# A state-space mixer computed by batch halves behind its convolution

## The reference, cut to what matters

```
z, xs, Bs, Cs, dt = split(h @ w_in.T);  xBC = silu(conv(xs, Bs, Cs) + b)
a = dt * A;  cs = cumsum(a) in chunks of 128 tokens;  L = exp(cs_q - cs_k), causal
Yd = (C B^T * L) (x dt)            # inside a chunk
states = sum_q exp(cs_end - cs) B (x dt);  S <- g S + states, S = 0 at each sequence's start
Yo = C S_prev exp(cs)              # from the chunks before
y = (Yd + Yo + D x) * silu(z);  h = res + y @ w_out.T
h2 = h * rsqrt(mean(h*h) + eps) * ln2_w;  h + (silu(h2 gate^T) * (h2 up^T)) down^T
```

## Time and profile before

| | before |
|---|---|
| median of three runs | 2204.54 us |
| profiled execution | 2204.26 us, span 2202.4 us |
| TensorE / weight loads / VectorE / ScalarE / POOL busy | 96 / 77 / 76 / 48 / 8 % |
| TensorE's mean granted clock | 0.981 |
| DMA | 361.6 MB, mean 164 GB/s |
| chain that ended last, by engine | PE 82 %, DVE 12 %, ACT 3 %, issue 2 %, DMA 1 % |

### The profile page before, as it was taken

The page is one execution under the profiler, slowest core; times in us unless marked ns, Lnnn a source line. Parts: engine busy times, 40 slices in busy tenths (PEclk is TensorE's granted clock), DMA queues, the critical chain, the costliest instruction groups (busy, mean ns, idle before and its releaser), DMA issues.

```text
span 2202.4 us, 26828 instructions
## 1 busy us (share of the span) xinstructions
PE 2123.8 (96%) x9262; PEld 1687.1 (77%) x9266; DVE 1668.0 (76%) x2498; ACT 1051.5 (48%) x1710; POOL 174.8 (8%) x287
## 2 busy tenths in 40 slices
PE   7999998969999999999999999799999999999999
PEld 3787776847888887888888864578888888888887
DVE  7775566468777888887978888977777777689885
ACT  4333224226777777776444456533333333334442
POOL 0000110000111111111000000200000000000000
PEclk9999999979999999999999999899999999999999
DMA  3151002525889999989360032634454444665201
GB/s 120 39 189 41 28 29 95 134 34 169 298 297 311 321 341 333 315 307 373 112 220 1 1 144 83 176 137 167 148 180 150 151 172 146 232 229 183 86 19 58
DMA packets 132958, 361.61 MB, mean 164 GB/s; under 512 B 16288, under 2 KB 27168, under 8 KB 129184
## 3 DMA queue, kind: packets, MB, share of 16 engines
q1 hardware_dynamic: 108912, 279.78, 37.1%
q0 software_dynamic: 23920, 80.23, 10.6%
HBM read 279.73 MB, written 84.41 MB: 165 GB/s over the span
## 4 chain that ended last, share of the span: by engine, by line
PE 82%; DVE 12%; ACT 3%; issue 2%; DMA 1%; DVEq 0%; SPq 0%; ACTq 0%
PE pair L913 41%; PE pair L938 24%; PE pair L718 9%; DVE conv_out L1873 1%; PE pair L969 1%; DVE comb_lo L1624 1%; DVE ring_lo L1574 1%; PE pair L831 1%; DVE pair L1710 1%; PE pair L856 1%; PE pair L857 1%; PE pair L838 1%; PE pair L754 1%; PE pair L860 1%; PE pair L963 1%
## 5 line engine op out<-in xcount | busy, mean ns | idle before, releaser
L913 PE MATMUL pair<-comb_hi,ring_hi 128*128 128x512 f32 x1568 | 618.4, 394 | 34.7 <-DVE comb_lo L1621 12.4
L913 PE MATMUL pair<-comb_hi,ring_lo 128*128 128x512 f32 x1568 | 615.6, 393 | 0.0
L913 PE MATMUL pair<-comb_lo,ring_hi 128*128 128x512 f32 x1568 | 615.6, 393 | 0.0
L913 PEld LDWEIGHTS pair<-comb_hi,ring_hi 128*128 128x128 f32 x1568 | 297.8, 190 | 106.8 <-issue 22.9
L913 PEld LDWEIGHTS pair<-comb_hi,ring_lo 128*128 128x128 f32 x1568 | 297.7, 190 | 62.5
L913 PEld LDWEIGHTS pair<-comb_lo,ring_hi 128*128 128x128 f32 x1568 | 298.2, 190 | 61.5
L938 PE MATMUL pair<-inner_ring_a,ring_hi 128*128 128x512 f32 x1120 | 344.9, 389 | 0.0
L938 PEld LDWEIGHTS pair<-inner_ring_a,ring_hi 128*128 128x128 f32 x1120 | 210.1, 188 | 43.6
L938 PE MATMUL pair<-inner_ring_a,ring_lo 128*128 128x512 f32 x560 | 217.9, 389 | 0.0
L1158 ACT ACTIVATE ring_hi<-ring_sum 128x512 fp32r<-128x512 f32 x168 | 106.0, 631 | 147.0 <-DVE ring_sum L1561 145.2
L718 PE MATMUL pair<-act_hi,weights_hi 128*128 128x512 f32 x416 | 138.6, 414 | 12.2 <-DVE act_lo L1517 8.0
(11 more groups left out here) (340 smaller groups left out, 3191.5 us busy)
## 6 DMA issues: line engine op xcount, KB each, us to landing
coeff_in<-f_gu SPq DMA_DIRECT2D x56, 512.0 KB, 5.2
coeff_in<-b_gu SPq DMA_DIRECT2D x56, 512.0 KB, 6.8
weights_raw<-w_mamba SPq DMA_DIRECT2D x28, 512.0 KB, 3.3
raw_a<-w_gu SPq DMA_DIRECT2D x28, 512.0 KB, 6.8
raw_a<-w_gu SPq DMA_DIRECT2D x56, 256.0 KB, 6.3
u_spill<-gate_a POOLq DMA_DIRECT2D x56, 256.0 KB, 6.0
coeff_in<-f_dn SPq DMA_DIRECT2D x28, 512.0 KB, 4.5
coeff_in<-b_dn SPq DMA_DIRECT2D x28, 512.0 KB, 6.3
```

The costliest lines, as they stand in the source:

```text
L913: ins = pe.matmul(out, wt[:, slot, col], a, start=t in (0, 1, 3) and kk == 0 and n == 0, stop=kk == KH - 1 and n == 2, skip_group_check=True)
```

## The change

Everything from the gate projection to the root works on one batch half at a time, batch 1 first (ORDER = (1, 0)).

- Each weight block of the gate and the output projection is loaded and split twice, once for each half: 32 positions instead of 16. A chunk has two half blocks of its own batch; TensorE's half_step does three matmuls of 512 columns.
- The first chunk of a sequence leaves out the state (no decayed C, no product with it; the state is a copy), the last leaves out the new state and the transposes of B. The hardware loops are written out, and the copies of columns into cur go.
- Gate activations of batch 1 are done in chunk 4, its products and splits in chunks 5 to 7 (Y_AT). Batch 0's are made during the output blocks of batch 1.
- The output projection has 16 half blocks on four PSUM banks; residual reload and x_sum stores are by halves too.
- Squares, their sum, root and scale are per half. Batch 1's sum is taken behind block 9, its root at block 10, combinations 0 and 1 at blocks 11 and 13, the first four ring weights at block 14. Batch 0's root comes behind the last block, with its sum between the first two products of the feed-forward.
- act_hi, act_lo, the gate and the combinations get other places in memory (T_HI, T_LO).

The diff, cut to its core; of the loops that are replaced only the new text stands here, moved to the left:

```diff
-N_CONV, N_Z, N_OUT, N_MLP = 0, CONV_TILES, CONV_TILES + 8, CONV_TILES + 16
+N_CONV, N_Z, N_OUT, N_MLP = 0, CONV_TILES, CONV_TILES + 16, CONV_TILES + 32
+BLOCK_OF = list(range(CONV_TILES)) + 2 * list(range(CONV_TILES, CONV_TILES + 8)) + 2 * list(range(CONV_TILES + 8, CONV_TILES + 16))
+ORDER = (1, 0)
+Y_AT = {5: (0, 1, 2), 6: (3, 4, 5), 7: (6, 7)}
...
-    AH = at("act_hi", 0, [P, KT, TOK], F32R)
-    AL = at("act_lo", 32 * KB, [P, KT, TOK], F32R)
+    AH = at("act_hi", 0, [P, BATCH, KT, H], F32R)
+    AL = at("act_lo", 32 * KB, [P, BATCH, KT, H], F32R)
...
-    zg = at("z_gate", R0, [P, KT, TOK], F32)
+    zg = (at("z_gate_a", R0 + 16 * KB, [P, KT, H], F32), at("z_gate_b", R0, [P, KT, H], F32))
+    rms_scale = at("rms_scale", R0 + 16 * KB, [P, BATCH, H], F32)
+    rms_sq = at("rms_squares", R0 + 20 * KB, [P, 2, H], F32)
+    rms_sum = at("rms_sum", R0 + 24 * KB, [P, BATCH, H], F32)
+    rms_t = at("rms_steps", R0 + 28 * KB, [P, BATCH, H], F32)
...
-    T_HI = ((56, 96, 104, 112, 120, 176, 184), (0, 24, 80, 32, 176, 184, 48))
-    T_LO = ((0, 8, 16, 24, 32, 40, 48), (16, 8, 88, 56, 72, 64, 40))
+    T_HI = ((0, 8, 16, 48, 112, 176, 96), (0, 24, 80, 32, 176, 184, 48))
+    T_LO = ((32, 40, 24, 56, 120, 184, 104), (16, 8, 88, 56, 72, 64, 40))
...
-with sp.Fori(0, (N_MLP - 4) // 2) as i:
-    for s in range(2):
-        load(i * 2 + (4 + s), s, w_mamba[i * 2 + (4 + s)])
+for n in range(4, N_MLP):
+    load(n, n % 2, w_mamba[BLOCK_OF[n]])
...
-pool.dma_start(hres[:, :, :], hs_spill.rearrange("k p t -> p k t")).then_inc(s_reload, 16)
+for h, b in enumerate(ORDER):
+    pool.dma_start(hres[:, :, HALF[b]], hs_spill.rearrange("k p t -> p k t")[:, :, HALF[b]]).then_inc(s_reload[h], 16)
 pool.wait_ge(s_xcopy, 16)
-for o in range(KT):
-    pool.wait_ge(s_h, o + 1)
-    pool.dma_start(x_sum[o], hres[:, o, :], accum_op=ALU.add).then_inc(s_xsum, 16)
+for h, b in enumerate(ORDER):
+    for o in range(KT):
+        pool.wait_ge(s_h, h * KT + o + 1)
+        pool.dma_start(x_sum[o][:, HALF[b]], hres[:, o, HALF[b]], accum_op=ALU.add).then_inc(s_xsum, 16)
...
+def half_step(out, wi, b, k):
+    for n, (w, a) in enumerate(((WH, ah), (WH, al), (WL, ah))):
+        ins = pe.matmul(out, w[:, wi, k * P:(k + 1) * P], a(b, k),
+                        start=k == 0 and n == 0, stop=k == KT - 1 and n == 2, skip_group_check=True)
+    if k == KT - 1:
+        ins.then_inc(s_used, 1)
...
+def gate_steps(q, first, last):
+    for u in range(first, last):
+        s, k = divmod(u, KT)
+        if k == 0:
+            pe.wait_ge(s_ready, N_Z + 2 * q + s + 1)
+            if q > 0:
+                pe.wait_ge(s_z, 2 * q - 1 + s)
+        half_step(bank(s), s, ORDER[q // CHUNKS], k)
+for q in range(NC):
+    h, c = divmod(q, CHUNKS)
+    b = ORDER[h]
+    first = KT if c == 0 else 4
+    gate_steps(q, 0, first)
+    pe.wait_ge(s_conv, CONV_TILES + 2)
+    pe.wait_ge(s_csx, 2)
+    pe.wait_ge(s_rr, q + 1)
+    for g in range(GROUPS):
+        ins = pe.matmul(ps[1][:, g * 512:(g + 1) * 512], ones[:, :], cs_rhs[:, g * HPG:(g + 1) * HPG, :],
+                        start=True, stop=False, skip_group_check=True)
+    ins.then_inc(s_cs, 1)
+    pe.wait_ge(s_bx, q + 1)
+    pe.wait_ge(s_silu, CONV_TILES)
+    pe.wait_ge(s_yt, q + 1)
+    for g in range(GROUPS):
+        pe.matmul(ps[2][:, g * 512:(g + 1) * 512], bx_cur[:, 2 + g, :],
+                  xbc[:, 4 + g * HPG:4 + (g + 1) * HPG, b * SEQ + c * P:b * SEQ + (c + 1) * P],
+                  start=True, stop=True)
+    gate_steps(q, first, first + 2)
+    if c > 0:
+        pe.wait_ge(s_state, h * (CHUNKS - 1) + c)
+    for j in range(4 if c < CHUNKS - 1 else 2):
+        ins = pe.transpose(ps[3][:, j * P:(j + 1) * P], bx_cur[:, j, :], ident)
+    ins.then_inc(s_stage, 1)
+    gate_steps(q, first + 2, first + 4)
+    if c > 0:
+        pe.wait_ge(s_ecs, h * (CHUNKS - 1) + c)
+    for g in range(GROUPS):
+        ins = pe.matmul(ps[1][:, g * 512:(g + 1) * 512], ident_bf[:, :],
+                        mask_bf[:, :].unsqueeze(1).to_broadcast([P, HPG, P]),
+                        start=False, stop=True, skip_group_check=True)
+    ins.then_inc(s_msk, 1)
+    gate_steps(q, first + 4, 2 * KT)
+    pe.wait_ge(s_att, q + 1)
+    for hd in range(HEADS):
+        ins = pe.matmul(ps[2][:, hd * P:(hd + 1) * P], x_dt[:, hd, :], att[:, hd, :], start=True, stop=c == 0)
+        if c > 0:
+            ins = pe.matmul(ps[2][:, hd * P:(hd + 1) * P], state[:, hd, :], c_dec[:, hd, :], start=False, stop=True)
+    ins.then_inc(s_y, 1)
+    if c < CHUNKS - 1:
         for g in range(GROUPS):
             ins = pe.matmul(ps[3][:, g * 512:(g + 1) * 512], b_tm[:, g, :], x_end[:, g * HPG:(g + 1) * HPG, :],
                             start=True, stop=True)
         ins.then_inc(s_st, 1)
+def rms_sums(h):
+    pe.wait_ge(s_sqd, (KT - 1) * (h + 1))
+    pe.matmul(bank(6 + h), ones[:, :], rms_sum[:, h, :], start=True, stop=True).then_inc(s_rv, 1)
+pe.wait_ge(s_z, 2 * NC)
+for n in range(BATCH * KT):
+    h, o = divmod(n, KT)
+    pe.wait_ge(s_ready, N_OUT + n + 1)
+    if n >= 4:
+        pe.wait_ge(s_h, n - 3)
+    for k in range(KT):
+        if o == 0:
+            pe.wait_ge(s_act, h * KT + k + 1)
+        half_step(bank(n % 4), n % 2, ORDER[h], k)
+    if n == KT + 1:
+        rms_sums(0)
+pe.wait_ge(s_yt, NC + 1)
...
+feed_forward(BASE_G[0], BASE_G[0] + 1)
+rms_sums(1)
+feed_forward(BASE_G[0] + 1, BASE_G[0] + 2)
+pe.wait_ge(s_h, BATCH * KT)
+feed_forward(BASE_G[0] + 2, W_END[0] - 4)
...
+def y_hi(h, k):
+    act.wait_ge(s_a, h * KT + k + 1)
+    act.activation(ah(ORDER[h], k), xbc[:, 4 + k, HALF[ORDER[h]]], ACT.Copy).then_inc(s_ah, 1)
+def z_silu(h, k):
+    act.wait_ge(s_z, h * KT + k + 1)
+    act.activation(zg[h][:, k, :], zg[h][:, k, :], ACT.Silu).then_inc(s_zs, 1)
+for q in range(NC):
+    h, c = divmod(q, CHUNKS)
+    col = ORDER[h] * CHUNKS + c
+    if c > 0:
         act.wait_ge(s_cs, q + 1)
         act.activation(c_dec[:, :, :], ps[1][:, :].rearrange("p (h q) -> p h q", h=HEADS), ACT.Exp).then_inc(s_ecs, 1)
+    act.wait_ge(s_msk, q + 1)
+    for hd in range(HEADS):
+        ins = act.activation(att[:, hd, :], ps[1][:, hd * P:(hd + 1) * P], ACT.Exp, bias=ncs_all[:, col, hd:hd + 1])
+    ins.then_inc(s_dec, 1)
+    for s in range(2):
+        act.wait_ge(s_used, N_Z + 2 * q + s + 1)
+        act.activation(zg[h][:, 2 * c + s, :], bank(s), ACT.Copy).then_inc(s_z, 1)
+        weights_hi(N_Z + 2 * q + s + 2, s)
+        if q == CHUNKS and s == 0:
+            for k in range(KT):
+                z_silu(0, k)
+    for k in Y_AT.get(q, ()):
+        y_hi(0, k)
+def rms_square(h, o):
+    act.wait_ge(s_h, h * KT + o + 1)
     if o >= 3:
+        act.wait_ge(s_sqd, h * (KT - 1) + o - 2)
+    elif h > 0:
+        act.wait_ge(s_sqd, KT - 1)
+    dst = rms_sq[:, o % 2, :] if o else rms_sum[:, h, :]
+    act.activation(dst, hres[:, o, HALF[ORDER[h]]], ACT.Square).then_inc(s_sq, 1)
+def rms_root(h):
+    act.preload_act_table_set("natural_log_exp_and_others")
+    act.wait_ge(s_rv, h + 1)
+    own.then(act.activation(rms_t[:, h, :], bank(6 + h), ACT.Ln, bias=EPS_COL, scale=1.0 / DM))
+    act.activation(rms_scale[:, h, :], rms_t[:, h, :], ACT.Exp, scale=-0.5).then_inc(s_hroot, 1)
+for n in range(BATCH * KT):
+    h, o = divmod(n, KT)
+    if N_OUT + n + 2 < N_MLP:
+        weights_hi(N_OUT + n + 2, n % 2)
+    if h == 0:
+        z_silu(1, o)
+        if o >= 1:
+            y_hi(1, o - 1)
+    elif o == 2:
+        rms_root(0)
+    elif o == 3:
+        comb_hi(0, 0)
+    elif o == 5:
+        comb_hi(0, 1)
+    elif o == 6:
+        for w in range(4):
+            weight_hi(w)
+    rms_square(h, o)
+    if n == KT - 1:
+        y_hi(1, KT - 1)
+for w in range(4, RING):
+    weight_hi(w)
+rms_root(1)
...
+def make_y(h, k):
+    y = xbc[:, 4 + k, HALF[ORDER[h]]]
+    dve.wait_ge(s_yt, CHUNKS * (h + 1) + 1)
+    dve.wait_ge(s_zs, h * KT + k + 1)
+    TT(y, y, zg[h][:, k, :], ALU.mult).then_inc(s_a, 1)
+def y_lo(h, k):
+    b = ORDER[h]
+    dve.wait_ge(s_ah, h * KT + k + 1)
+    TT(al(b, k), xbc[:, 4 + k, HALF[b]], ah(b, k).bitcast(F32), ALU.subtract).then_inc(s_act, 1)
+for q in range(NC):
+    h, c = divmod(q, CHUNKS)
+    b = ORDER[h]
+    tok = slice(b * SEQ + c * P, b * SEQ + (c + 1) * P)
+    col = b * CHUNKS + c
+    if c > 0:
+        dve.wait_ge(s_ecs, h * (CHUNKS - 1) + c)
         TT(c_dec[:, :, :], c_dec[:, :, :], xbc[:, 4:4 + HEADS, tok], ALU.mult)
+    dve.wait_ge(s_stage, q + 2)
+    if c < CHUNKS - 1:
         dve.tensor_copy(b_tm[:, :, :], ps[3][:, 256:512].rearrange("p (g n) -> p g n", g=GROUPS))
+    for g in range(GROUPS):
+        heads = slice(g * HPG, (g + 1) * HPG)
+        ins = TT(x_dt[:, heads, :], ps[3][:, g * P:(g + 1) * P].unsqueeze(1).to_broadcast([P, HPG, P]),
+                 dt_all[:, col, heads].unsqueeze(2).to_broadcast([P, HPG, P]), ALU.mult)
+    own.then(ins)
+    if c < CHUNKS - 1:
+        TT(x_end[:, :, :], x_dt[:, :, :], dend_all[:, col, :].unsqueeze(2).to_broadcast([P, HEADS, P]), ALU.mult)
```

(73 more changed lines are left out.)

246 lines of the change are left out of this document (40 added, 206 removed).

## The result

The changed kernel takes **2175.3 us** (median of 4 runs, 2173.06 to 2177.41) beside 2204.55 of the kernel before on the same chip (2200.02 to 2205.87): ratio 0.9871, 95% interval [0.9854, 0.9887], 29.2 us less. The forecast was 2180 with 2169 to 2192. The profiled execution took 2173.49 us with a span of 2171.7, so it lies 1.8 under the median.

A forecast was written before the change was run, and what follows sets the result against it. TensorE, busy 96% of the span, was taken to bound the kernel. Terms -7.4 - 10.1 + 3.0 + 1.3 + 0.5 - 11.5 = -24.2 us took 2204.26 + 0.3 to 2180.4, said as 2180, range 2169 to 2192.

The forecast's parts named there:

- Chunks: First and last chunks: state products and two of four transposes left out, twice 3.68 us, all on the path: -7.4 us.
- First hole: From the chunks' end to the output projection's end: 97.1 us, of which its matmuls need 87.0: -10.1 us.
- Late tile: Second batch's act_lo for tile 7, needed by output block 8, comes 1.7 us late; taken as +3.0 us.
- Reload: Residual reload split in two on POOL's queue, first half landing in 7.5 to 15.0 us: 0, with +6 as the end.
- Weights twice: 16 more 512 KB weight loads on SP's queue, with 8.4 us allowed and 3.2 to land: cost 0.
- Root's sum +1.3, block 14 +0.5: Output projection: sum matmul between blocks 9 and 10, +1.3 us; VectorE's load around block 11 delays a weight split, +0.5.
- Second hole: From the projection's end to steady ring matmuls: third combination starts 14.1 us behind the projection, not 25.65: -11.5 us.
- Table load: ScalarE's table switches take 1.28 us without drain; with the skill's 1.38 us drain the kernel would take 2184.
- A: Rival, last five output blocks: VectorE overloaded, root and third combination at most 3 us earlier, 2189 us; chance 0.20.
- B: Rival: blocks 8 and 14 don't wait, second table load dropped, ring splits overlap, 2173 us; chance 0.20.
- C: Rival, output projection: ScalarE and VectorE need 6.5 us a half block, not 5.2; about 2200 us; chance 0.04.
- D: Rival, second weight fetch: loads landing later than 8.4 us make each of 16 output blocks wait, 2222 at 11 us; chance 0.06.

The follow-up runs named there:

- run 1: Changed kernel with stand-ins of the same shape for the state products and transposes left out in first and last chunks: 2184.1 us, ratio 0.9914.
- Run 4: Changed kernel with batch 1's gate products, act_hi and act_lo all made behind the last chunk, as before: 2184.39 us, ratio 0.9914.
- Run 5: Changed kernel with tile 7's act_hi and act_lo of batch 0 made ahead of block 7's residual add and square: 2173.7 us.
- run 11: Changed kernel with two extra 512 KB memory-to-memory transfers behind each weight load of the output projection: 2182.58 us, ratio 0.9903.
- run 10: Changed kernel with one extra 512 KB memory-to-memory transfer behind each weight load of the output projection: 2176.99 us, ratio 0.9875.
- Run 6: Changed kernel without the second table load, in front of batch 0's root: 2172.73 us, ratio 0.9858.
- run 3: Changed kernel with combinations 0 and 1 made behind batch 0's root again, not at blocks 11 and 13: 2183.53 us, ratio 0.9907.
- Run 8: Changed kernel with two more half-width VectorE additions in front of each residual add of blocks 0 to 7: 2187.83 us, ratio 0.9931.
- run 2: Kernel before with only the state products of first and last chunks left out, transposes kept: 2195.99 us, against 2203.15 in the same measurement.
- run 9: Changed kernel with one more VectorE half addition behind each gate product and split of blocks 0 to 7: 2180.85 us, ratio 0.9897.

## Why the prediction was right

- **Chunks, -7.4: right.** -7.6 in the traces once the entry's clock is out, +7.5 when undone (run 1). Each sequence of four chunks lost 3.8 us. No wait arose in chunk 5, and the cover there was wider than worked out. The exponential is done at 296.87, 3.5 us ahead of the mask matmul, where the prediction had 0.8. The first and last chunks do not show as 19 and 18.8 between two running-sum matmuls, as the prediction said they would. They show as 17.1 to 17.3 and 21.4, since gate steps of the next chunk lie on one or the other side of the mark; before, they showed as 18.9 (second sequence) and 23.4, so 1.8 and 2.0 went.
- **First hole, -10.1: right.** The projection starts (350.89) 0.14 us behind the start of the chunks' last product, without a wait. Run 4 shows the cause: with the activations late, 5.46 us of wait and 2.8 of clock come back, 8.3 of the 8.9 us.
- **Late tile, +3.0: mis-sized on the safe side.** The working had 1.7 and I took 3.0 for a late VectorE and a lower clock. The wait was 1.42, VectorE was not late, and the clock stayed at 1.00 behind it. Run 5 prices the whole at 1.7.
- **Reload, 0: right.** The first half's add waited 1.19 us for it at 361.68, and TensorE for nothing. The 0 was partly luck: the half that is needed first took 10.1 us, not the 7.5 of the sum, but it was issued 0.6 us into block 0 and not 3.6, so the add came at 10.8 us, near the 11.8 of the sum. The second half took 16.0 us, more than the 15.0 taken as the end, and nothing waited for it. In run 11, with the add at 14.2 us behind the projection's start, the formula of the prediction (add to split 3.1, needed at 16.3) gives a wait of 1.0, where 1.24 was measured.
- **Weights twice, 0: right.** Twice the traffic of the second fetch cost nothing in the stretch (run 10), three times did (run 11).
- **Root's sum +1.3, block 14 +0.5: right.** From the sum matmul's start to the next regular pair are 1.1 us; the wait at block 14 was 0.25. Run 5's projection, where the late tile is gone, takes 1.7 us more than the 87.0 of its matmuls; 1.8 were forecast for the two.
- **Second hole, -11.5: 1.3 short.** VectorE and ScalarE were through the last squares and ring splits 1.2 us sooner than listed: the last addition of squares ended 5.6 us behind the projection in place of 6.5, ScalarE's last split at 8.0 in place of 9.2. The chain behind it took the times listed for it. The first ring product didn't wait 2.6 us for its split, but 1.92, for nothing that the profile names. VectorE's first ring split started at 442.46 and takes about 0.7, so it ends 0.1 before the product starts; that it released the product is likely, not shown.
- **Table load.** The traces show no drain at a switch: in chunk 5 the load from the gate's activation back to the exponential (294.55) starts 0.02 us behind the end of ScalarE's last operation, and the exponential starts 0.02 us behind the load's end. Run 6, which leaves out the load in front of batch 0's root, gains 1.4 in the trace, the load's own 1.28 and no more; there the same tables were in already. The Trainium skill (ScalarE: Activation LUTs, section "What ACT_TABLE_LOAD costs") adds 1.38 us of drain to each switch to a different set; here the measurement differs and decides. By it, as an estimate, two drains would be 2.8 us, and chunk 5's cover of 3.5 us would have held them, where the prediction had it lose 2 us.

**The rivals.** A (second hole stays) fell: 12.8 us went; run 3 shows what it would have looked like if the combinations had stayed. B (better) had the direction: the late tile and the hole were better than taken, though block 8 did wait and the table load stayed; its 2173 lies 2.3 us under the 2175.3 measured, the forecast 4.7 above. The truth is inside the forecast's own range, 2174 to 2186, and near its lower end. C's chain per block is 4.7 us, not the 5.2 that I had worked out, let alone 6.5. Run 8, at 6.13, confirms C's price for the blocks (0.68 x 8 less 2.94 of lead is 2.5; some 2.7 were seen) and shows that C lacked its dearer part, the last two tiles and the clock. D's price was off: with three times the traffic it came first through the reload, then through four late weight loads and the clock, 6.8 us in the stretch and not a wait at each block. At the traffic of the change the median weight load took 3.6 us and the longest, beside the reload, 7.5, which is 0.9 under the 8.4.

The sum came out at -24.2 where the traces have -27.1 from the change; the missing 2.9 are the late tile (1.3 to 1.6) and the second hole (1.3). The rest up to 29.2 I count as difference between executions; no run shows more of it. Between the terms all errors point the same way, so none hid another in the sum.

## What to carry to other kernels

Cutting a stage into two halves paid twice here, because its head and its tail both left the main engine idle: the other half fills the holes, and only the halves' seams are left. A part of the gain, 7.6 of 27.1 us, has nothing to do with the halves: it is work on a zero or unused state that is left out, and run 2 gets most of it in the kernel before. Before cutting a stage, work out the chain of one piece on the helper engines against the main engine's time for it; here 0.7 us per block were left, and one more 0.7 us operation cost 3.7 us in the stretch. Price an idle TensorE as its wait plus what its clock may lose behind it, and work out the cover of every transfer: in run 11 the largest broke first, and the frequent ones cost more.

## What the runs showed that I had not expected

- The same wait does not always bring the same clock. The 2.23 us in front of the chunks stands in all 13 traces; in 5 of them the next four matmul records took 3.5 to 3.7 us, in 8 they took 1.98 or 1.99. The stretch from 100 to 120 us, the same work in all, had a mean clock of 0.97 in the trace of before, 0.91 in the changed kernel's and 0.86 in run 9's. All 13 traces follow one pattern: the 5 with the half clock at the entry had 0.97 to 0.99 there, the other 8 had 0.84 to 0.93. So a low clock can turn up at one place instead of another. With the code in front of the chunks the same in its work, the chunks began anywhere from 196.04 to 199.21 us, a difference of up to 3 us between single traces that no edit explains.
- A wait of 1.42 us left the clock at 1.00; waits of 0.90 and 2.26 us, 3.2 us apart, were followed by 9 us at 0.81, and one of 5.46 us by 5.7 us at half.
- Work left out right in front of a hole buys nothing: of run 2's 7.0 us the last 1.72 went into the hole.
- In run 11 the DMA share reads 1.02 with 339 GB/s from 378 to 400 us; weight loads of 512 KB landed in 6.5 us in the median, and in 8.2 to 9.9 at the worst. In the kernel before, the share reads 1.05 with 215 GB/s in the earlier trace rows. So a full share doesn't say what rate can be had, and the 280 GB/s of the lone reload, which I took as the limit for run 11, was none.
